# A macaron block on one NeuronCore: more FFN chunks on split operands, hidden rows read by tokens for the first layer norms, the last expert finished in two halves

## What is computed

```python
x = L0_attn_hidden_states                                # (2, 1024, 128)
x = x + 0.5 * _L0_ffn_ref(_layernorm(x, axis=-1), router_w, w1, b1, w2, b2)
x = x + _L0_attn_ref(_layernorm(x, axis=-1), ...)
x = x + 0.5 * _L0_ffn_ref(_layernorm(x, axis=-1), router_w, w1, b1, w2, b2)

# _L0_ffn_ref: 8 experts, the 2 best of each token by softmax weight
h = relu(einsum('tc,efc->tef', x, w1) + b1)              # C = 128, F = 512
y = einsum('tef,ecf->tec', h, w2) + b2
out = einsum('tkc,tk->tc', the two chosen y, their weights, normalised)

# _L0_attn_ref: token shift, r, w, k, v, g by low-rank mixes of x, then over time
kv = k_t[..., :, None] * v_t[..., None, :]               # 4 heads, K 16, V 32
o_t = einsum('bhk,bhkv->bhv', q_t, S + u * kv)
S = exp(-exp(w_t))[..., None] * S + kv
# group norm of o, times silu(g), times W_o
```

## Time and profile before

| what | value |
|---|---|
| median of 3 runs | 503.16 us (502.64 to 503.83) |
| the profiled execution | 504.78 us |
| its span, first to last instruction | 503.0 us |
| mean granted TensorE clock | 0.993 of full |
| PE busy | 488.5 us, 97% of the span |
| DVE, ACT, POOL busy | 65%, 62%, 45% |

### The profile page before, as it was taken

The page is one execution under the profiler, slowest core; times in us unless marked ns, Lnnn a source line. Parts: engine busy times, 40 slices in busy tenths (PEclk is TensorE's granted clock), DMA queues, the critical chain, the costliest instruction groups (busy, mean ns, idle before and its releaser), DMA issues.

```text
span 503.0 us, 6055 instructions
## 1 busy us (share of the span) xinstructions
PE 488.5 (97%) x1822; PEld 294.8 (59%) x1822; DVE 327.8 (65%) x647; ACT 309.6 (62%) x529; POOL 224.9 (45%) x245
## 2 busy tenths in 40 slices
PE   6999999999999999999999999999999999999996
PEld 2766666555556556554654655555566555677774
DVE  2455156939974784996477799933759992366653
ACT  3566568576555657664565775545776564487873
POOL 1043341437873261875516157724525873331323
PEclk9799999999999999999999999999999999999999
DMA  7093110129510015940003544111026611003200
GB/s 227 25 352 111 42 39 4 43 90 235 161 38 23 1 43 150 227 126 1 1 3 126 146 149 146 63 64 42 0 90 195 179 63 42 1 0 109 82 0 21
DMA packets 20575, 43.52 MB, mean 87 GB/s; under 512 B 3776, under 2 KB 3904, under 8 KB 20544
## 3 DMA queue, kind: packets, MB, share of 16 engines
q1 hardware_dynamic: 14208, 31.61, 20.2%
q10 hardware_dynamic: 6336, 11.54, 7.9%
...
## 4 chain that ended last, share of the span: by engine, by line
PE 82%; issue 6%; DVE 5%; ACT 3%; POOL 3%; POOLq 0%; ACTq 0%; DVEq 0%
PE Y L329 28%; PE U L308 11%; PE U L310 10%; PE U L309 10%; PE A L398 3%; PE Y L324 2%; PE Y L325 2%; PE Y L326 2%; PE A L390 2%; PE A L384 1%; ACT xnt L497 1%; PE A L355 1%; POOL xT L847 1%; PE A L338 1%; PE Y L333 1%
## 5 line engine op out<-in xcount | busy, mean ns | idle before, releaser
L525 ACT ACTIVATE hid<-U,small 128x512 f32<-128x512 f32 x188 | 129.0, 689 | 119.1 <-PE U L310 118.5
L329 PE MATMUL Y<-hid,w 128*128 128x512 f32 x376 | 191.8, 591 | 0.0
L308 PE MATMUL U<-xhi,w1lo 128*128 128x512 f32 x256 | 169.5, 662 | 1.1 <-issue 0.6
L847 POOL TENSOR_TENSOR xT<-xT,gy 128x512 f32<-128x512 f32 x64 | 82.8, 1294 | 160.6 <-DVE gy L727 160.6
L310 PE MATMUL U<-xhi,w1hi 128*128 128x512 f32 x256 | 101.7, 397 | 0.0
L309 PE MATMUL U<-xlo,w1hi 128*128 128x512 f32 x256 | 100.9, 394 | 0.0
L308 PEld LDWEIGHTS U<-xhi,w1lo 128*128 128x128 f32 x256 | 48.7, 190 | 65.2 <-issue 56.3
L868 POOL TENSOR_TENSOR qs<-q,pool_a 128x512 f32<-128x512 f32 x64 | 75.9, 1187 | 17.6 <-DVE pool_a L755 17.6
L329 PEld LDWEIGHTS Y<-hid,w 128*128 128x128 f32 x376 | 70.7, 188 | 16.1
L718 DVE TENSOR_TENSOR hid_lo<-hid,hid_hi 128x512 fp32r<-128x512 f32 x68 | 54.0, 801 | 28.0 <-ACT hid_hi L523 27.6
L309 PEld LDWEIGHTS U<-xlo,w1hi 128*128 128x128 f32 x256 | 49.1, 192 | 39.4 <-issue 37.4
...
## 6 DMA issues: line engine op xcount, KB each, us to landing
...
```

The lines of the kernel that those rows point to most:

```text
L308: mm(dst, w1lo[:, e, f, :], xhi[:, k % NB, :], start=True, stop=False)
L329: mm(dst, w2[:, g % E, f, :], hid[:, n % HS, :], start=first, stop=final).then_inc(down, 1)
L525: act.activation(hid[:, n % HS, :], U[n % 2][:, :], ACT.Relu, bias=bias).then_inc(h_f, 1)
L847: pool.tensor_tensor(xT[:, h, b, :], xT[:, h, b, :], gy[:, g % 2, :], ALU.add).then_inc(acc, 1)
```

## The change

1. `in_parts` also takes three chunks of four in block 0 from expert 1 on (21 chunks), one chunk of four beside the scans (31 chunks), and the six chunks 208 to 214 behind the last unit's scans. 126 chunks are in parts now, 130 are plain.
2. The hidden rows of the first four groups come a second time from DRAM, laid out by tokens (`tokens_in`), straight into the layer norm's tile `xnt`. For them `to_tokens` is gone, `stats` and `normalise` read SBUF, and in the first layer norm VectorE normalises two of the four tiles. `prepare` waits for the bank at its step `T_CHN`, four slots later than before.
3. The first up-projection of a block waits for `xlo` in front of its second matmul.
4. In block 0 VectorE rounds w1 (from expert 2 on), and GpSimd rounds w2 and subtracts (expert 1 first, expert 0 last). Routing of block 0 is spread over slots 1 to 3. The weights of experts 4 to 7 are issued ahead of the routing weights' DMAs.
5. The last expert is combined, added and stored in two halves, by VectorE and SP alone (`finish`).

```diff
 def in_parts(n):
 
-    scans = any(slot_of(i, T_SC) - 3 <= n < slot_of(i, T_OUT) for i in range(UNITS))
-    return n >= SLOTS and n % FC < FP and not scans
+    scans = any(slot_of(i, T_SC) - 3 <= n < slot_of(i, T_PO if i == UNITS - 1 else T_OUT) for i in range(UNITS))
+    return n >= FC and n % FC < (1 if scans else FP)
...
+            def tokens_in(k):
+                at = LN_FFN[k] % 2 * 4
+                if LN_FFN[k] >= 2:
+                    sp.wait_ge(ln_T, LN_FFN[k] - 1)
+                sp.dma_start(xnt[:, at:at + 4, :].rearrange("p t n -> p (t n)"), xtok_in[:, k * NT:(k + 1) * NT]).then_inc(tok_in[k], 16)
...
-            rows_in(0)
+            tokens_in(0)
             sp.dma_start(ident, const_in[:, C_ID:C_ID + P]).then_inc(id_l, 16)
             sp.dma_start(w(W_RT, W_ALL - W_RT), small_in[:, W_RT:W_ALL]).then_inc(vec_l, 16)
             weights(0)
             weights(1)
             sp.dma_start(const[:, C_ID + P:C_ALL], const_in[:, C_ID + P:C_ALL]).then_inc(const_l, 16)
-            rows_in(1)
             for e in range(2, 4):
+                weights(e)
+            tokens_in(1)
+            rows_in(0)
+            for e in range(4, E):
                 weights(e)
             gates_to_rows(0)
             for c in range(GS // EQ):
                 gates_in(0, c)
-            for e in range(4, E):
-                weights(e)
-            rows_in(2)
+            for k in range(1, UNITS):
+                rows_in(k)
+            tokens_in(2)
             sp.dma_start(w(0, W_RT), small_in[:, 0:W_RT]).then_inc(small_l, 16)
-            rows_in(3)
...
+            rows_out(6)
+            h, b = home(7)
+            for c in range(2):
+                at = slice(c * NT // 2, (c + 1) * NT // 2)
+                sp.wait_ge(fin, c + 1)
+                sp.dma_start(ov[:, h, b, at], xT[:, h, b, at]).then_inc(out_done, 16)
+            sp.wait_ge(out_done, 80)
...
                 if f == 0 and e == 0:
                     pe.wait_ge(xn_hi, k + 1)
-                    pe.wait_ge(xn_lo, k + 1)
                 if k == 0 and f == 0:
                     pe.wait_ge(w1hi_s, e + 1)
                     pe.wait_ge(w1lo_s, e + 1)
                 dst = U[n % 2][:, :]
                 mm(dst, w1lo[:, e, f, :], xhi[:, k % NB, :], start=True, stop=False)
+                if f == 0 and e == 0:
+                    pe.wait_ge(xn_lo, k + 1)
                 mm(dst, w1hi[:, e, f, :], xlo[:, k % NB, :], start=False, stop=False)
                 mm(dst, w1hi[:, e, f, :], xhi[:, k % NB, :], start=False, stop=True).then_inc(up, 1)
...
@@ -318,8 +343,8 @@
                 dst, first, final = Y[g % 2][:, :], f == 0, f == FC - 1
                 if in_parts(n):
                     at = PARTS.index(n) % PS
-                    if g < 2 * E:
-                        pe.wait_ge(w2lo_s, g % E + 1)
+                    if g <= E:
+                        pe.wait_ge(w2lo_s, g)
                     pe.wait_ge(h_lo, parts_to(n + 1))
                     mm(dst, w2lo[:, g % E, f, :], hid_hi[:, at, :], start=first, stop=False)
...
                 for t in range(4):
+                    if ln == 0 and t == 2:
+                        pe.wait_ge(ln_dve, 1)
                     last = pe.transpose(bank[:, t * P:(t + 1) * P], xnt[:, ln % 2 * 4 + t, :], ident)
...
             def prepare(k, t):
 
-                if t == 0:
-                    if k < UNITS:
-                        pe.wait_ge(x_in[k], 16)
-                    else:
-                        pe.wait_ge(x_att, k - UNITS + 1)
+                if t == (T_CHN if k < UNITS else 0):
                     pe.wait_ge(lg_sub, k)
                     if SCANNED[k]:
                         pe.wait_ge(o_r, SCANNED[k])
+                if t == 0 and k >= UNITS:
+                    pe.wait_ge(x_att, k - UNITS + 1)
                     to_tokens(A[3], k)
                 if t == T_CHN:
...
-            pe.wait_ge(x_in[0], 16)
-            to_tokens(A[0], 0)
             keep_clock(2)
             to_channels(0, A[0])
             keep_clock(1)
...
             def normalise(ln, bank):
                 act.wait_ge(ln_rst, ln + 1)
-                for t in range(4):
+                for t in range(4 if ln else 2):
                     at = ln % 2 * 4 + t
-                    last = act.activation(xnt[:, at, :], bank[:, t * P:(t + 1) * P], ACT.Identity,
+                    src = xnt[:, at, :] if ln in LOADED else bank[:, t * P:(t + 1) * P]
+                    last = act.activation(xnt[:, at, :], src, ACT.Identity,
                                           bias=shift[:, at:at + 1], scale=rstd[:, at:at + 1])
...
-                if n % 4 == 0 and n // 4 + 1 < E:
-                    split_w1(n // 4 + 1)
+                if n == 0:
+                    split_w1(1)
                 if n == 0:
                     experts_exp(0)
-                if n % 4 == 2 and 1 <= n // 4 <= E:
-                    split_w2(n // 4 - 1)
...
             def split_w1(e):
+                if e >= 2:
+                    dve.wait_ge(w1_in[e], 16)
+                    dve.tensor_copy(w1hi[:, e].rearrange("p f n -> p (f n)"), w1raw[:, e, :]).then_inc(w1hi_s, 1)
                 dve.wait_ge(w1hi_s, e + 1)
                 dve.tensor_tensor(w1lo[:, e].rearrange("p f n -> p (f n)"), w1raw[:, e, :],
                                   w1hi[:, e].rearrange("p f n -> p (f n)"), ALU.subtract).then_inc(w1lo_s, 1)
 
             def stats(ln, bank):
-                dve.wait_ge(ln_src, ln + 1)
                 t0 = ln % 2 * 4
+                if ln in LOADED:
+                    dve.wait_ge(tok_in[LOADED.index(ln)], 16)
+                else:
+                    dve.wait_ge(ln_src, turned(ln))
                 for t in range(4):
-                    last = dve.bn_stats(bst[:, t0 + t, :], bank[:, t * P:(t + 1) * P])
+                    src = xnt[:, t0 + t, :] if ln in LOADED else bank[:, t * P:(t + 1) * P]
+                    last = dve.bn_stats(bst[:, t0 + t, :], src)
...
+            def finish():
+
+                g = BLOCKS * E - 1
+                h, b = home(BLOCKS - 1)
+                dve.wait_ge(down, (g + 1) * FC)
+                dve.wait_ge(acc, g)
+                for c in range(2):
+                    at = slice(c * NT // 2, (c + 1) * NT // 2)
+                    link(dve.scalar_tensor_tensor(out=gy[:, g % 2, at], in0=Y[g % 2][:, at], scalar=w(W_B2 + g % E, 1),
+                                                  in1=G[:, g % GS, at], op0=ALU.add, op1=ALU.mult))
+                    dve.tensor_tensor(xT[:, h, b, at], xT[:, h, b, at], gy[:, g % 2, at], ALU.add).then_inc(fin, 1)
...
-            stats(0, A[0])
+            stats(0, None)
             dve.wait_ge(vec_l, 16)
             link(dve.tensor_copy(rwh[:, 0, :], w(W_RT, E)))
             dve.tensor_tensor(rwh[:, 1, :], w(W_RT, E), rwh[:, 0, :], ALU.subtract).then_inc(rw_r, 1)
             scales(0)
+            for t in (2, 3):
+                last = dve.tensor_scalar(xnt[:, t, :], xnt[:, t, :], mv[:, t, 0:1], rstd[:, t:t + 1],
+                                         ALU.subtract, ALU.mult)
+            last.then_inc(ln_dve, 1)
             split_w1(0)
...
                 if n == 1:
                     dve.wait_ge(const_l, 16)
-                    for step in range(1, 6):
+                if 1 <= n < 4:
+                    for step in ((1, 2), (3, 4), (5,))[n - 1]:
                         route(0, step)
...
             split_h(ALL - 1)
-            combine(BLOCKS * E - 1)
+            finish()
...
             def add_y(g):
                 h, b = home(g // E)
                 pool.wait_ge(comb, g + 1)
+                if g % E == 0 and g // E < UNITS:
+                    pool.wait_ge(x_in[g // E], 16)
                 if g >= 1:
...
             def split_w2(e):
-                pool.wait_ge(w2hi_s, e + 1)
+
+                done = (e - 1) % E + 1
+                pool.wait_ge(w2_in[e], 16)
+                pool.tensor_copy(w2hi[:, e].rearrange("p f n -> p (f n)"),
+                                 w2[:, e, 0:FP].rearrange("p f n -> p (f n)")).then_inc(w2hi_s, 1)
+                pool.wait_ge(w2hi_s, done)
                 pool.tensor_tensor(w2lo[:, e].rearrange("p f n -> p (f n)"), w2[:, e, 0:FP].rearrange("p f n -> p (f n)"),
                                    w2hi[:, e].rearrange("p f n -> p (f n)"), ALU.subtract).then_inc(w2lo_s, 1)
...
-                if n % 4 == 3 and 1 <= n // 4 <= E:
-                    split_w2(n // 4 - 1)
+                if n % 4 == 0 and n // 4 < E:
+                    split_w2((n // 4 + 1) % E)
                 for i in range(UNITS):
                     attend(i, step_of(i, n))
-            add_y(BLOCKS * E - 1)
```

19 lines of the change are left out of this document (10 added, 9 removed).

## The result

| kernel | median us | runs | ratio to before, 95% interval |
|---|---|---|---|
| before | 503.50 | 4 (502.64 to 504.06) | |
| changed | 510.75 | 4 (510.29 to 511.73) | 1.0147 (1.0127 to 1.0166) |

The change makes the kernel 1.5% slower. 501.8 was forecast, with a range up to 508: the sign is wrong and the time is outside the range. One execution of e11, a kernel further down, took 542.63 us at a mean granted clock of 0.852, and is left out of all numbers. The profiled execution of the changed kernel took 511.73 us, its span is 509.9, 6.9 more than before.

A forecast was written before the change was run, and what follows sets the result against it. The prediction took TensorE as the bound, with VectorE nearly so beside the scans. Its terms summed to -1.4 us, a span of 501.6 and a forecast of 501.8 us, range 496 to 508.

The forecast's parts named there:

- The start (-2.6): Up to the first up-projection: earlier statistics, tiles split over two engines and a later wait for xlo save 2.6 us.
- its clock (-1.7): First four slots: a shorter idle gap keeps TensorE's clock full, 5.35 us in place of 7.04, saving 1.7.
- Block 0 in parts (-3.4): In block 0, 21 chunks in parts save 0.16 us each, 3.4 in sum.
- its waits (+1.3, bounded at 3): In block 0, TensorE waits for VectorE near block 1's routing, next w1 and second layer norm: +1.3 us (0 to 3).
- 20 small instructions at 0.19 to 0.22: VectorE's small instructions in the routing of block 1, slots 13 to 16, counted as 4.2 us.
- GpSimd's rounding of w2 "hidden": In block 0, GpSimd's added rounding costs nothing, as it has under 4 us of work in four slots.
- Beside the scans (+9.1): At the four units, subtractions of 0.6 us between VectorE's scans make the last reduces later, +9.1 us in sum.
- up to 3 us per unit: Expected sign at the reduces: TensorE waits this long in each unit for a GpSimd product.
- The 16 other chunks (-2.6): Chunks in parts behind the units' last scans and 208 to 214 save 0.16 us each, 2.6 in sum.
- End (-0.4): At the program's end, the second store has half the data, saving 0.4 us (0 to 1).
- (a): Rival: VectorE's additions beside the scans find cover; 489.4 us in full (chance 0.08), 495 to 499 in part (0.15).
- (b): Rival: subtractions beside the scans meet running GpSimd work, 0.9 us more each; 508 to 520 us, chance 0.20.

The follow-up runs named there:

- e11: Changed kernel with no chunk in parts beside the units and GpSimd's rounding and subtraction of w2 for experts 4 and 5 moved early; 497.4 us.
- e8: Changed kernel without one pair of keep_clock matmuls on zeros ahead of the first transposes; 513.21 us.
- e10: Changed kernel with GpSimd rounding and subtracting w2 of experts 4 and 5 right behind expert 3, earlier than the routing; 508.09 us.
- e6: Changed kernel without VectorE's subtraction for chunks in parts beside the scans, that part of the result left uncomputed; 500.26 us.
- e5: Changed kernel with one chunk, 124, plain instead of in parts; 506.71 us.
- e1: Changed kernel with no chunk in parts from 3 slots before a unit's scans to its end; 499.75 us.
- e12: Changed kernel with two chunks of four in parts beside the units instead of one; 531.02 us.

## Why the prediction was wrong, point by point

- **The start (-2.6) and its clock (-1.7).** Right: first up-projection 2.55 earlier, slot 4 4.30 earlier, and e8 shows what idle time does there by putting some back. (TensorE's own row had 2.87 us of idle time ahead of 9.88 in the kernel before; the forecast's "over 3" was taken from the weight load.) But the clock term holds for the profiled pair and hardly for the medians. Of the 28 executions of the kernel before that ran beside the experiments, 20 show a mean clock of 0.999 or 1.000 and spans of 500.3 to 501.2 us, where the profiled one has 0.993 and 503.0. Most of them probably had no such fall (they left no trace, so this is not shown). The forecast set its median 0.16 above the profiled span, while each of these executions takes 1.8 to 3.0 us more than its own span. Without the clock term it would have been 503.5 in place of 501.8.
- **Block 0 in parts (-3.4) and its waits (+1.3, bounded at 3).** The first term was right in size (away from the routing, slots in parts follow each other at 1.39 us, as forecast, for instance at 37.14 and 38.53 in e10), the second is the step that failed. The load of VectorE was counted as "20 small instructions at 0.19 to 0.22", each at the price that it has alone, read from a group whose eight instructions all met nothing. The trace of the kernel before had two neighbours of that group at 1.06 and 0.93 beside GpSimd. Now four of them met GpSimd and cost 2.6 us more than that price. Waits, clock and what follows came to about 5, where 3 was the bound. The contention was weighed, but only for the subtractions. GpSimd's add and its subtraction of w2 lay beside that routing before, too (1.6 us); the change put its rounding of w2 there as well, and the subtractions for chunks in parts behind the routing.
- **GpSimd's rounding of w2 "hidden".** GpSimd had the time, as said. It was VectorE that paid for it.
- **Beside the scans (+9.1).** Right, unit by unit, with the mechanism and the price of 0.6 per subtraction: 8.9 measured, and taking away only the subtractions (e6) gives 10.5 back. The waits look different from the forecast's "up to 3 us per unit" at the reduces: there are ten of them, the longest 1.4, 6.4 in sum. Part of that sum is not at the reduce, where the forecast had put all of it, but at down-projections in parts that wait for their own subtraction (0.63, 2.27 and 0.98 us at units 1 to 3).
- **The 16 other chunks (-2.6).** Chunk 124 was among the "three behind each of units 0 to 2" that should save 0.16 each. The forecast looked behind each unit's last scan only for what the subtraction adds, and not for what is queued behind it while it waits: ScalarE has the normalising of a layer norm (1.5 us) ahead of the relu there, and VectorE's program holds the last steps of unit 1 behind the subtraction. Cost: 4.0 us (e5), of which about 1.6 is the clock behind the longer wait.
- **The clock after the start** had no term at all. Three falls of 3.4 us each (behind 42.5, 260.4 and 305 us) stand in the profiled execution. Such a stretch at half the clock does the work of 1.7, so each costs up to 1.7 us (1.4 for the first and 1.6 for the second, against traces without the fall), and they are part of the sums for the stretches above. The four runs with mean clocks of 0.990 and 0.993 differ by about 1 us (511.05 and 511.73 against 510.29 and 510.45), which fits one fall more or less.
- **End (-0.4)**: about -0.5, right.

Of the rivals, (a), cover for the additions, is excluded by e1 and e12. (b), GpSimd holding the port, was looked for at the wrong instructions: the subtractions beside the scans come first, as the forecast argued, and GpSimd pays. Where (b) did come true is the routing in block 0 and, in e12, the second of two subtractions in a row. The Trainium skill (page "SBUF — State Buffer", section "Who interferes with whom") says that a VectorE instruction with two SBUF inputs and a GpSimd instruction that reads SBUF lock each other out, and that "Issue order, not op shape, decides who blocks." The trace agrees on both sides: 0.19 to 1.07 for a 128x32 instruction that came second, 0.18 to 0.56 for GpSimd's copy of one column. The forecast took the rule to set one price and did not run it over the small instructions, for which it is by far the dearest.

So the forecast's terms as they stood, with the 4.0 more that block 0 took and the 3.85 more of slots 119 to 131, make -1.4 + 7.85 = +6.45 of the 6.9 measured in the span; these two places are the error.
